# Second attention layer: the transposed row maxima in bank 4, and the masked keys made by GpSimd

## The reference

```
x = x + tanh(g_xattn[0]) * attention0(layernorm(x), ctx, ctx)
x = x + tanh(g_ffn[0])   * experts(layernorm(x))          # 64 experts, top 8, and a shared one
x = x + tanh(g_xattn[1]) * attention1(layernorm(x), ctx, ctx, mask)
x = x + tanh(g_ffn[1])   * quantised_ffn(layernorm(x))
```

## Time and profile before

| | |
|---|---|
| median of 3 runs | 1977.8 us (1976.33 to 1977.88) |
| the profiled execution | 1975.05 us, of which the span 1973.3 us |
| busy in the span | PE 1735.6, PEld 1370.3, DVE 1413.0, ACT 1156.0, POOL 565.4 us |
| chain that ended last | PE 60%, DVE 20%, issue 7%, DMA 5%, POOL 5% |

### The profile page before, as it was taken

One profiled execution on the slowest core, in us unless ns is written; L12 is line 12 of the kernel. 1 busy time (PEld: TensorE's weight loads), 2 busy tenths in 40 slices (PEclk: granted clock), 3 DMA queues, 4 the chain that ended last, 5 costly groups with the idle time before them and its releaser, 6 DMA issues.

```text
span 1973.3 us, 53907 instructions
## 1 busy us (share of the span) xinstructions
PE 1735.6 (88%) x20198; PEld 1370.3 (69%) x20208; DVE 1413.0 (72%) x4651; ACT 1156.0 (59%) x2347; POOL 565.4 (29%) x552
## 2 busy tenths in 40 slices
PE   5999999999999997688887886599999999978855
PEld 4888888888888885467666765466666666643334
DVE  4788788878887886465444443488888788759988
ACT  3666666666666663122222221588888888858875
POOL 1000000000000000488888888211111111111147
PEclk9999999999999998799999999799999999989989
DMA  3122222221222241788888886322222222203265
GB/s 103 46 64 63 65 66 66 69 69 61 66 61 69 61 120 52 202 215 209 220 211 209 210 211 131 92 67 66 77 66 67 75 68 66 67 26 139 117 230 197
DMA packets 194481, 214.04 MB, mean 108 GB/s; under 512 B 25584, under 2 KB 170352, under 8 KB 192048
## 3 DMA queue, kind: packets, MB, share of 16 engines
q1 hardware_dynamic: 169408, 171.97, 27.2%
q0 software_dynamic: 24816, 38.62, 10.4%
HBM read 125.63 MB, written 84.89 MB: 107 GB/s over the span
## 4 chain that ended last, share of the span: by engine, by line
PE 60%; DVE 20%; issue 7%; DMA 5%; POOL 5%; ACT 1%; SPq 1%; POOLq 0%; DVEq 0%; ACTq 0%
DVE mt L835 8%; PE tiles L378 7%; PE tiles L361 7%; PE bank L444 6%; PE bank L524 6%; PE bank L476 6%; PE bank L487 4%; PE bank L408 3%; PE bank L547 3%; PE bank L456 3%; DMA xr<-token_rows,tid 3%; PE tiles L345 3%; DVE hmax L1714 2%; POOL accumulator L1501 2%; POOL xr L1486 2%
## 5 line engine op out<-in xcount | busy, mean ns | idle before, releaser
L1973 POOL TENSOR_TENSOR rstd<-var,minus_half 128x2 f32<-128x2 f32 x139 | 97.0, 698 | 900.8 <-DVE var L914 887.7
L835 DVE TENSOR_REDUCE mt<-tiles 128x16 f32<-128x2048 f32 x128 | 293.5, 2293 | 82.4 <-PE tiles L361 82.4
L608 ACT ACTIVATE pt<-tiles 128x2048 f32<-128x2048 f32 x128 | 240.7, 1881 | 48.7 <-PE tiles L378 48.7
L1501 POOL DMA_INDIRECT accumulator<-ye,tid x128 | 204.9, 1601 | 47.0 <-issue 33.4
L1446 DVE TENSOR_SCALAR ye<-bank,xr 128x256 f32<-128x256 f32 x128 | 56.1, 479 | 195.2 <-PE bank L1336 129.0
L1486 POOL DMA_INDIRECT xr<-token_rows,tid x128 | 139.4, 1089 | 73.3 <-DVE within L1414 34.3
L444 PE MATMUL bank<-xt,w_q 128*128 128x128 f32 x1024 | 154.3, 284 | 0.9 <-ACT xt L616 0.9
L361 PE MATMUL tiles<-qkp 32*128 32x256 f32 x2048 | 149.4, 405 | 3.2 <-ACT qkp L630 3.0
L378 PE MATMUL tiles<-qm,qkp 32*128 32x128 f32 x4096 | 150.2, 283 | 1.4 <-DVE mt L835 1.4
L378 PEld LDWEIGHTS tiles<-qm,qkp 32*128 32x128 f32 x4096 | 125.8, 186 | 27.3 <-issue 24.6
L444 PEld LDWEIGHTS bank<-xt,w_q 128*128 128x128 f32 x1024 | 131.1, 194 | 14.8 <-issue 13.1
(11 more groups left out here) (246 smaller groups left out, 4099.4 us busy)
## 6 DMA issues: line engine op xcount, KB each, us to landing
keys_values<-res SPq DMA_DIRECT2D x64, 256.0 KB
cxax<-accumulator SPq DMA_DIRECT2D x128, 128.0 KB, 2.3
cxax<-keys_values SPq DMA_DIRECT2D x128, 128.0 KB, 2.5
hidden_away<-h_ring SPq DMA_DIRECT2D x8, 1536.0 KB, 5.1
token_rows<-pay SPq DMA_DIRECT2D x64, 160.0 KB, 1.8
pt<-in_expert_up SPq DMA_DIRECT2D x36, 256.0 KB
cxax<-in_ctx SPq DMA_DIRECT2D x64, 128.0 KB, 2.2
res<-in_x SPq DMA_DIRECT2D x64, 128.0 KB, 2.2
```

The costliest lines, as they stand in the source:

```text
L608: nc.scalar.activation(pt[r % 2][:, :, :], tiles[:, :, :], ACT.Exp).then_inc(sem("exp_done"), 1)
L835: nc.vector.tensor_reduce(mt[:, :].rearrange("p (i n c) -> p i n c", i=RT, n=2 * KC)[:, :, :, 0], tiles[:, :, :].rearrange("p i (n k) -> p ...
L1501: nc.gpsimd.indirect_dma_start(out=acc[p][:, :], out_offset=bass.IndirectOffsetOnAxis(ap=tid[b % 8][:, h:h + 1], axis=0), in_=ye[r][:, h, ...
```

## The change

In the second layer `maxima_t` writes to columns 256 to 383 of bank 4 and waits for ACT's copies `xt` in place of DVE's residual. The transposes of rows wait for the `qm` of the slot before, and the output no longer waits for `qm`. `mask_keys` leaves ACT; POOL makes the same four pieces per block with `tensor_scalar`, between its power and its bias addition, and raises a new semaphore `keys_masked`, for which the scores and SP's loads of keys wait. In ACT's order the values go first and the second normalisation stands before the first.

```
--- before.py
+++ after.py
@@ -328,6 +328,7 @@
             slots(body, NB, first, NB + LAGS)
 
         FIRST = (-1, -3)
+        MAXC = (0, D)
 
         MOE_IN = 16 * 9
         MASKS_IN = MOE_IN + 16 * 2 * RT
@@ -353,6 +354,7 @@
                 wait(pe, "exp_done", first + b - 1)
                 if L == 1:
                     masks(0)
+                    pe.wait_ge(sem("keys_masked"), b + 1)
                 for j in range(KC):
                     pe.wait_ge(sem(sm("qk_out")), 2 * b + j + 1)
                     for i in range(RT):
@@ -389,9 +391,8 @@
                     pe.wait_ge(sem(sm("xt_out")), ahead(b, 2))
                     wait(pe, sm("silu_done"), b - 3)
                 else:
-                    wait(pe, sm("x3_done"), b - 2)
-                bk = bank[4 if L == 0 else 6]
-                nc.tensor.transpose(bk[:, 0:P], mt[:, :], ident[:, :]).then_inc(sem("mt_done"), 1)
+                    pe.wait_ge(sem(sm("xt_out")), ahead(b, 3))
+                nc.tensor.transpose(bank[4][:, MAXC[L]:MAXC[L] + P], mt[:, :], ident[:, :]).then_inc(sem("mt_done"), 1)
 
             def values(k):
 
@@ -420,6 +421,7 @@
                     pe.wait_ge(sem(sm("v_out")), b + 1)
                 else:
                     wait(pe, sm("xt_out"), b)
+                    pe.wait_ge(sem("qm_done"), first + max(b - 2, 0))
                 for c in range(KC):
                     last = nc.tensor.transpose(bank[4][:, c * P:(c + 1) * P], xn[p][:, c * P:(c + 1) * P], ident[:, :])
                 last.then_inc(sem(sm("t_done")), 1)
@@ -466,7 +468,6 @@
                 if L == 0:
                     wait(pe, sm("x2t_out"), b)
                 else:
-                    pe.wait_ge(sem("qm_done"), first + ahead(b, 3))
                     wait(pe, sm("x3_done"), b)
                 if L == 0 and b == 0:
                     pe.wait_ge(sem("made_step"), made("biases0", 9))
@@ -631,17 +632,6 @@
                                                     bias=kb[:, e, j:j + 1], scale=keep[:, e:e + 1])
                     last.then_inc(sem(sm("qk_out")), 1)
 
-            def mask_keys(f):
-                if f is None:
-                    return
-                b, r = f
-                p = r % 2
-                act.wait_ge(sem(f"kv_in{p}"), 16 * (b - p) + 32)
-                wait(act, "st_done", first + b - 3)
-                for j in range(KC):
-                    for e in range(2):
-                        nc.scalar.activation(kp[r][:, e, j, :], kvt[p][:, j * P:(j + 1) * P], ACT.Identity, bias=kb[:, e, j:j + 1], scale=keep[:, e:e + 1])
-
             def copy_v(f):
                 if f is None:
                     return
@@ -750,12 +740,11 @@
                     gate_tanh(w)
                     copy_ov(k)
                 else:
-                    mask_keys(f)
+                    copy_v(f)
+                    normalise_second(u)
                     normalise_first(g)
-                    normalise_second(u)
                     copy_ov(o)
                     copy_qk(f)
-                    copy_v(f)
                     copy_xt(g)
                     exponent(k)
                     copy_at(o)
@@ -845,7 +834,7 @@
                 wait(dve, "st_done", first + b)
                 for e in range(2):
                     last = nc.vector.scalar_tensor_tensor(qm[:, e, :, :],
-                                                          bank[4 if L == 0 else 6][:, 0:P].unsqueeze(1).broadcast_to([P, KC, P]),
+                                                          bank[4][:, MAXC[L]:MAXC[L] + P].unsqueeze(1).broadcast_to([P, KC, P]),
                                                           keep[:, 1 - e:2 - e], qt[r % 2][:, :, :], ALU.mult, ALU.add)
                 last.then_inc(sem("qm_done"), 1)
 
@@ -1132,7 +1121,7 @@
                     return
                 b, r = n
                 p = r % 2
-                wait(sp, sm("qk_out"), 2 * (b - 1))
+                wait(sp, "keys_masked", b - 1)
                 wait(sp, sm("v_out"), b - 1)
                 sp.dma_start(kvt[p][:, 0:D].rearrange("p (c t) -> p c t", c=KC),
                              keys_values[b - p].rearrange("p (c e t) -> p c e t", c=KC, e=2)[:, :, p, :]).then_inc(sem(f"kv_in{p}"), 16)
@@ -1938,6 +1927,7 @@
             sp.wait_ge(sem("sum_done_1"), NB)
             sp.wait_ge(sem("t_done_1"), NB)
             sp.wait_ge(sem("qk_out_1"), 2 * NB)
+            sp.wait_ge(sem("keys_masked"), NB)
             sp.wait_ge(sem("v_out_1"), NB)
             for n, w in enumerate((wgi, wui, wdi)):
                 sp.dma_start(w[:, :, :].rearrange("p a b -> p (a b)"), ffn_int[n]).then_inc(sem("ffn_int_in"), 16)
@@ -1981,8 +1971,20 @@
             phase_end(pool, 2)
             experts_pool(pool)
             phase_end(pool, 3)
+            def mask_keys(b):
+                r, p = b % 4, b % 2
+                pool.wait_ge(sem(f"kv_in{p}"), 16 * (b - p) + 32)
+                wait(pool, "st_done", NB + b - 3)
+                for j in range(KC):
+                    for e in range(2):
+                        last = G.tensor_scalar(kp[r][:, e, j, :], kvt[p][:, j * P:(j + 1) * P], keep[:, e:e + 1], kb[:, e, j:j + 1],
+                                               ALU.mult, ALU.add)
+                last.then_inc(sem("keys_masked"), 1)
+
             for s in range(NB + PAIR[1]):
                 inverse_roots(pool, 1, s)
+                if 1 <= s <= NB:
+                    mask_keys(s - 1)
                 if s < NB:
                     pool.wait_ge(sem("xn1_done_1"), s + 1)
                     G.tensor_tensor(row(s), row(s), bias[:, :], ALU.add).then_inc(sem("biased_1"), 1)
```

More of the change, by code:

```diff
@@ L632, in copy_qk @@
                     last.then_inc(sem(sm("qk_out")), 1)
[L634 to L643, removed]
             def copy_v(f):
```

## The result

The changed kernel took 1953.57 us (median of 4 runs, 1953.15 to 1957.6) against 1977.84 before (4 runs, 1976.33 to 1978.39): ratio 0.9883, 95% interval 0.9866 to 0.9900. On a second chip it took 1956.11 against 1976.54: 0.9885 (0.9866 to 0.9904). The forecast was 1956.4.

What follows compares the result with a forecast made beforehand. No engine is full; the order of waits bounds the kernel, with the transposed maxima waiting for VectorE's residual. 61 slots x 0.35 = 21.4 us, so 1977.8 - 21.4 = 1956.4 us; range 1952 to 1968, the forecast's own 1953 to 1960.

Steps and rivals of the forecast that it cites:

- The slot: Second layer's steady attention: row maxima 7.47 us apart in place of 7.82, a gain of 0.35 a slot.
- The transpose of the maxima: On TensorE, in bank 4 it no longer waits for VectorE's residual and starts 0.45 us sooner, 0.27 behind the heads' transposes.
- What is late next: ScalarE's exponent releases the second masks, 3.54 us after the first masks, so a slot gains 0.35, not 0.45.
- TensorE's room behind it: Before the second masks TensorE could start at 1413.96 against the exponent's 1414.06: 0.10 us of room.
- ScalarE's masks: Four operations leave ScalarE, 1.65 us a slot; worth nothing by itself, since ScalarE waits for its transposed scores anyway.
- VectorE's room: Before the next row maxima VectorE keeps 0.17 us, nearly a second bound; were it the bound, the slot would be 7.30.
- the start of the shifted queries: On VectorE, after the residual and statistics: at 1414.52, with the small operation following at 1415.32.
- GpSimd's masks: Four added operations a slot between power and bias addition, 0.35 us each, hidden entirely, two slots before the scores read them.
- The slower rival: GpSimd's masks hold VectorE's small operation and the maxima behind it; at 1.06 us each, slot 8.70, time 2031; chance 0.09.
- the case that the prediction had priced at 0.2 only: VectorE's small operation gets in between two GpSimd masks (at 1.06 us each): only 0.2 us is lost.
- The fill: First slots, waiting for loads, TensorE's low clock and the power: put at zero, within 1 us either way.

Runs made afterwards that it cites:

- the repeat: The changed kernel once more with no edit, on the chip of the other three experiments: 1956.11 us, ratio 0.9885.

## Why the prediction was right, and where its sizes were off

**The slot.** Predicted 7.47, measured 7.467. The steady part gave 21.24 for the 60 distances (predicted 21.0). The 0.27 behind the heads and the 3.54 from first masks to second were both read off one slot of the old trace in which the waited-for thing did not yet exist, and that is why the slot fits to a hundredth (1404.67 to 1408.21 is 3.54 again).

**The transpose of the maxima.** Predicted 0.27 behind the heads' transposes and 0.45 sooner; measured 0.28 (1407.61 to 1407.89), and 5.56 after its maxima where it was 6.01. That the wait and nothing else held it is shown by the kernel that keeps it.

**What is late next.** The exponent, as predicted. TensorE's room behind it was put at 0.10 and is 0.125, shown by halving the exponent.

**ScalarE's masks.** "Worth nothing by itself" holds, from both sides: without the move all of the gain is there, with the move alone none. ScalarE waits 1.00 before its exponent after the move [in rows 4 it was 0.69].

**VectorE's room was mis-sized**: predicted 0.17, measured 0.30 idle before the maxima. The term that failed is the start of the shifted queries, taken over as 6.35 behind the maxima (1414.52 less 1408.17). They stood there because they too waited for the transpose: it ended at 1414.18 + 0.30 = 1414.48. With it 0.45 sooner they follow the statistics directly, 0.35 behind their start, and L907 starts 7.02 after the maxima, not 7.15 as the prediction wrote. Were VectorE the bound, the slot would be 7.17; the halved exponent agrees, 7.34 less its 0.17. It did not matter here since the exponent bounds first.

**GpSimd's masks** take 0.453 each and follow one another by 0.44, not 0.35. They end at 1408.36, 0.99 before L907: hidden, as predicted. The prediction gave them two slots before the scores read them; it is one: the group that ends at 1400.89 is read by the scores from 1408.58, 7.7 later. With three times the masks 3.3 of that are left.

**The slower rival** had a place and a price, and its place was tried: with eight and twelve operations GpSimd works on all through L908, as a mask of 0.9 and 1.3 us would, and the slot stays 7.47. Its price was that the maxima wait for GpSimd's whole row (8.70 at a mask of 1.06). That mechanism did not show in any of the 116 slots looked at: where the small operation was held, it was until the end of the one mask in progress, the case that the prediction had priced at 0.2 only. So its 0.09 was too much. Single masks of that length were not tried.

**The fill** was put at zero within 1 us. From the stage's fill came +1.47, of TensorE's clock, in this execution and none in the repeat: the bound was too tight for one execution. The median of the first chip moved by 24.3 where the spans differ by 21.7; the old kernel's profiled execution was 2.8 below its median and the new one's 0.2. On the second chip the medians differ by 20.4. The forecast of 21.4 lies between the two. The 2.9 that the first chip's medians moved beyond it stand in no part of the traces; what the traces show of the change is the 21.2 of the steady part, so that 1956.4 was right for the slot and missed the median of 1953.6 by less than executions of this kernel differ (1953.15 to 1957.6 on the first chip, 1948.51 to 1957.56 on the second).

## What to carry to other kernels

When a pipeline has filled for a few slots only, some slot often lacks one of the stages; what moves in that slot, and what releases the next step there, is a free experiment on the wait that one would remove, and it gives the next bound too. Two results that share a memory bank share their waits: look for a bank whose other user is long done. Work taken off an engine that waits anyway is worth nothing, but moving it is harmless as long as it fits the receiving engine's idle time.

## What the runs showed that I had not expected

VectorE's small operation with two SBUF inputs mostly ran in its usual 0.15 in the middle of GpSimd's row of twice the masks (median 0.151 of 58, longest 0.298); with three times the masks it took longer more often than not (median 0.230, longest 0.425). Two meetings of the kernel with twice the masks, each operation by itself:

```profile
1407.77 0.48 POOL L1984 TENSOR_SCALAR qkp<-cxax,keep,kb 128x128 f32<-128x128 f32 x1
1407.94 0.15 DVE L908 SCALAR_TENSOR_TENSOR nmr<-mv,rstd 128x2 f32<-128x2 f32 x1
```

```profile
1310.66 0.45 POOL L1984 TENSOR_SCALAR qkp<-cxax,keep,kb 128x128 f32<-128x128 f32 x1
1310.83 0.30 DVE L908 SCALAR_TENSOR_TENSOR nmr<-mv,rstd 128x2 f32<-128x2 f32 x1
```

In the first the small operation passes and the mask is 0.03 longer than the usual 0.447. In the second the mask has its usual length and the small operation ends 0.02 after it. The 116 meetings of the two kernels are of these kinds, but for 15 in which the small operation starts 0.33 or more into the mask and neither takes longer. In 56 the mask is the longer one (0.467 to 0.500) and the small operation ends at least 0.16 before it; in 45 the small operation is held and ends 0.004 to 0.035 after the mask, at most 0.28 late.

The Trainium skill (SBUF — State Buffer, Who interferes with whom) says that such an instruction contends with a GpSimd one that reads SBUF, and that the shared ports are an exclusive lock; of VectorE's two-port modes it says that whoever issues first has them for its whole instruction. By that L908 would have ended after the mask each time, at 1408.25 or later in the first meeting. The 45 agree, and so does L914 in the earlier trace rows; the 56 do not, and the measurement decides: there the mask had started first and L908 still went through in its middle. What decides between the two was not found: both kinds have starts of 0.17 into the mask.

The exponent costs 0.86 for each 1024 columns with 0.16 beside it (1.88 and 1.02), of which a second operation behind the first adds 0.06. And the sixteen masks, each 0.39 long in the trace, start within 0.05 of one another: where a queue comes to a wait is read from starts, not from lengths.
